# Last batch of a decoder block: expert picks moved among the cross scores, the cross query sent in parts, the last expert unit added by a one-hot product

## The reference, cut to what matters

```python
x = _layernorm(x + attn(x, ...))                       # 16 heads, low-rank q and kv, rope
x = _layernorm(x + xattn(x, ctx, ctx, mask, ...))      # q = x @ W0.T + b0, 16 heads of 16
# ffn, per batch b and expert e:
probs = softmax(einsum('bsd,ed->bse', x, choice_w))
G, I = top_k(swapaxes(probs, -1, -2), S * 2 // E)      # 256 tokens of each expert
h = silu(einsum('bekd,edf->bekf', take(x, I), w1))
out = zeros_like(x).at[b_idx, I].add(G[..., None] * einsum('bekf,efd->bekd', h, w2))
x = _layernorm(x + out)
```

## Time and profile before

| what | us |
|---|---|
| three runs | 1750.33, 1752.80, 1753.03 (median 1752.8) |
| profiled execution, its own time | 1750.27 |
| its span, first to last instruction | 1748.5 |
| mean granted TensorE clock | 0.943 of full |
| PE busy | 1545.2 (88%) |
| DVE busy | 1232.0 (70%) |
| ACT busy | 862.5 (49%) |
| POOL busy | 405.4 (23%) |

### The profile page before, as it was taken

One profiled execution on the slowest core, in us unless ns is written; L12 is line 12 of the kernel. 1 busy time (PEld: TensorE's weight loads), 2 busy tenths in 40 slices (PEclk: granted clock), 3 DMA queues, 4 the chain that ended last, 5 costly groups with the idle time before them and its releaser, 6 DMA issues. The chain is left out here.

```text
span 1748.5 us, 25995 instructions
## 1 busy us (share of the span) xinstructions
PE 1545.2 (88%) x9190; PEld 737.6 (42%) x9198; DVE 1232.0 (70%) x2551; ACT 862.5 (49%) x1611; POOL 405.4 (23%) x529
## 2 busy tenths in 40 slices
PE   7599998897999888989998989899986778999992
PEld 2222224544232255342222554322224436888872
DVE  5588854886888857888887677888865636664442
ACT  3167784353777733537777344477762231111121
POOL 5220001600200015002000250120000303666663
PEclk9699999898999998999999989899997888999997
DMA  6400001544100016350000172300002014555595
GB/s 186 124 12 1 1 2 37 153 97 104 37 1 1 1 37 183 72 135 1 1 2 29 37 191 67 105 1 2 1 1 72 23 50 123 110 111 115 111 257 120
DMA packets 101133, 118.72 MB, mean 68 GB/s; under 512 B 20365, under 2 KB 91021, under 8 KB 99853
## 3 DMA queue, kind: packets, MB, share of 16 engines
q1 hardware_dynamic: 85804, 95.81, 19.2%
q0 software_dynamic: 14208, 19.94, 6.5%
q10 hardware_dynamic: 992, 1.32, 0.3%
HBM read 65.62 MB, written 31.35 MB: 55 GB/s over the span
## 5 line engine op out<-in xcount | busy, mean ns | idle before, releaser
L1151 ACT ACTIVATE pT<-banks 128x512 f32<-128x512 f32 x1184 | 652.3, 599 | 290.5 <-PE banks L1986 165.1
L1465 DVE TENSOR_REDUCE nmf<-banks 128x1 f32<-128x1024 f32 x512 | 601.7, 1218 | 111.0 <-PE banks L1904 110.2
L1986 PE MATMUL banks<-qst,kst 99*128 99x512 bf16 x1024 | 344.2, 386 | 6.3 <-DVE nmf L1465 6.3
L1904 PE MATMUL banks<-kst,qst 96*128 96x512 bf16 x1024 | 311.7, 386 | 31.2 <-DMA qst<-oT 20.0
L2024 PE MATMUL banks<-pT,V 128*32 128x512 f32 x2048 | 274.3, 607 | 15.5 <-ACT oT L1139 12.3
L1986 PEld LDWEIGHTS banks<-qst,kst 99*128 99x128 bf16 x1024 | 96.1, 97 | 276.3 <-ACT pT L1151 173.2
L896 POOL CAST nmp<-nmf 128x16 bf16<-128x16 f32 x64 | 12.6, 196 | 774.1 <-issue 708.7
L1904 PEld LDWEIGHTS banks<-kst,qst 96*128 96x128 bf16 x1024 | 94.6, 99 | 152.2 <-DVE nmf L1465 44.6
L1321 ACT ACTIVATE kst<-banks 128x512 f32<-128x512 f32 x64 | 38.1, 597 | 204.7 <-PE banks L2350 204.6
L948 POOL DMA_INDIRECT acc_rows<-kst,tok_s x64 | 103.4, 1615 | 45.7 <-DMA acc_rows<-kst,tok_s 17.3
L1430 DVE STREAM_TRANSPOSE head_blocks<-oT 128x512 f32<-128x512 f32 x64 | 45.1, 705 | 89.5 <-ACT oT L1139 89.5
(11 more groups left out here) (244 smaller groups left out, 2168.2 us busy)
## 6 DMA issues: line engine op xcount, KB each, us to landing
qst<-q_parts SPq DMA_DIRECT2D x36, 256.0 KB, 5.1
kst<-k_parts SPq DMA_DIRECT2D x36, 256.0 KB, 7.8
qst<-in_w SPq DMA_DIRECT2D x16, 512.0 KB, 4.7
qxs<-in_w SPq DMA_DIRECT2D x16, 512.0 KB, 4.9
qst<-oT SPq DMA_DIRECT2D x60, 128.0 KB, 2.5
qxs<-oT SPq DMA_DIRECT2D x48, 128.0 KB, 2.5
xb<-in_x SPq DMA_DIRECT2D x4, 1024.0 KB, 6.8
x_rows<-z SPq DMA_DIRECT2D x4, 1024.0 KB, 8.8
```

Of the source, the lines that this page charges most:

```text
L1151: act.activation(pT[:, n % RING_P, :], PS[:, banks[what, n], :], ACT.Exp, scale=scale).then_inc(s_ex, 1)
L1465: dve.tensor_reduce(nmf[:, m % 2, j, t:t + 1], scores.rearrange("p a n -> p (a n)"), AX.X, ALU.max, negate=True).then_inc(s_smu, 1)
L1904: ins = pe.matmul(pair[:, half, :], qst[0:KQ, h, t * P:(t + 1) * P], kst[0:KQ, h, half * N:(half + 1) * N], start=True, stop=True)
L1986: ins = pe.matmul(ps, kst[0:KM, head, kc * P:(kc + 1) * P], qst[0:KM, head, cols], start=True, stop=True)
```

## The change

In the last batch: triple 0 is no longer chosen and picked ahead of cross attention. `choose` of triple 0 comes after the last "smax", its pick after "st" 21, its transposition after "st" 24; triple 1 is chosen after "st" 21, picked after "st" 31 and transposed after "st" 35. All picks use bank 1. On POOL the three gathers go behind the last split of the cross maxima. `rank_chosen` on PE goes between the cross queries 2 and 3; the subtractions of pieces 2 and 3 go into `ORDER_LAST` behind "smax" 1 and 3 (as batches 0 to 2 had them). SP sends the cross query part by part: three DMAs of a piece once its first part is taken, two at the second, one at the third.

At the end: unit 31 is not scattered. SP loads the sum of batch 3 after seven scatters, in two halves. POOL writes the token numbers 3072 to 4095 into `tokens` after unit 25, DVE compares them with the tokens of unit 31 (`spread`, two compares of 128 x 1024 after units 29 and 30), PE multiplies the one-hot tiles with the gated rows of unit 31 into banks 0 to 3 (`add_last`, 16 matmuls of 256 columns), and DVE adds the banks to the loaded sum, half by half, with statistics, power and norm by half. `hidden` of unit 31 goes behind `expert_out` of unit 30.

```diff
-ORDER_LAST = (ORDER_CROSS[:LAST_MAX + 25] + [("pick", 1)] + ORDER_CROSS[LAST_MAX + 25:LAST_MAX + 33]
-              + [("pick turned", 1)] + ORDER_CROSS[LAST_MAX + 33:])
+AFTER_ST = {21: ("pick", 0), 24: ("pick turned", 0), 31: ("pick", 1), 35: ("pick turned", 1)}
+for step in ORDER_CROSS:
+    ORDER_LAST.append(step)
+    if step == ("smax", SM_CROSS - 1):
+        ORDER_LAST.append(("choose", 0))
+    if step[0] == "st" and step[1] in AFTER_ST:
+        ORDER_LAST.append(AFTER_ST[step[1]])
+    if step == ("st", 21):
+        ORDER_LAST.append(("choose", 1))
...
 # SP, last batch
-                    for i in range(4):
-                        load_cross(i)
+                    for pair in ((0, 1), (2, 3)):
+                        for part in range(3):
+                            for i in pair:
+                                load_cross_part(i, part)
+                def load_cross_part(i, part):
+                    if part < 2:
+                        wait_apart(sp, s_xt[i], 2 * b + part + 1)
+                    else:
+                        wait_apart(sp, s_eva, at.taken("A", at.nth("qx", i) + 1))
+                    for t, term in enumerate(TERMS):
+                        if term[0] == part:
+                            sp.dma_start(rows[t:KQ:len(TERMS), :, half * N:(half + 1) * N],
+                                         xparts_at[:, i, part, :]).then_inc(s_qx[i], 16)
 # POOL: the three gathers behind split_max(..., range(4, NG)) instead of behind split_max(..., range(1))
 # ACT: cross parts in the order pair (0, 1), parts 0 1 2, then pair (2, 3)
 # DVE: route_early ends after routing_places
-                for n in range(SLOTS):
-                    choose(n)
-                take_rows(0)
-                take_choice(0)
-                scatter_tokens(0)
 # PE
+                        if order in (ORDER_AHEAD, ORDER_LAST) and n in (1, 3):
                             for i in (2, 3):
                                 subtract(at, b, i, n // 2)
...
                     cross_query(2)
+                    rank_chosen(EARLY * E, EARLY * TURNS + 2)
+                    subtracted((0, 1), 1)
                     cross_query(3)
-                    subtracted((0, 1), 1)
-                    subtracted((2, 3), 0)
-                    subtracted((2, 3), 1)
-                    rank_chosen(EARLY * E, EARLY * TURNS + 2)
-                    pick(0)
-                    pick_turned(0)
 # the end: SP
+                sp.wait_ge(s_sc[b], (E if b < EARLY else E - 1) * 32)
+                    for half in range(2):
+                        tiles = slice(half * T // 2, (half + 1) * T // 2)
+                        sp.dma_start(fin[b][:, tiles, :], rows[:, tiles, :]).then_inc(s_ah[half], 16)
 # POOL
+                if n < LAST:
+                    scatter(n)
+                if n == SPREAD_FROM - 4:
+                    pool.iota(tokens, pattern=[[1, S]], base=EARLY * S, ...)
 # DVE
+            def spread_rows(j):
+                dve.tensor_scalar(spread[:, j, :], tokens, tokf[:, 2 * k + j:2 * k + j + 1], None, ALU.is_equal)
+            def add_last(half, meanwhile=None):
+                dve.wait_ge(s_ah[half], 16)
+                for bank in (2 * half, 2 * half + 1):
+                    dve.wait_ge(s_fa, bank + 1)
+                    link_r(dve.tensor_tensor(fin[b][:, two, :], PS[:, bank, :]..., fin[b][:, two, :], ALU.add))
+                    for t in (2 * bank, 2 * bank + 1):
+                        ins = dve.bn_stats(st6[:, t, :], fin[b][:, t, :])
+                    if meanwhile is not None and bank % 2 == 0:
+                        meanwhile()
+                ...  # bn_aggr x4, + EPS, then POOL's power of the half
 # PE
+                for bank in range(4):
+                    for i in range(2):
+                        t = 2 * bank + i
+                        for j in range(2):
+                            ins = pe.matmul(PS[:, bank, i * D:(i + 1) * D], spread[:, j, t * P:(t + 1) * P],
+                                            yg[k][:, j, :], start=(j == 0), stop=(j == 1))
+                    ins.then_inc(s_fa, 1)
```

More of the change, by code:

```diff
@@ L205 @@
 UNITS = B * E
+LAST = UNITS - 1
+SPREAD_FROM = LAST - 2
 SLOTS = 3
@@ L208 @@
 WEIGHTS = 4
+PICK_BANK = 1
 def unit(n):
@@ L487, in decoder_block @@
         s_al = [sem(f"sum_loaded{i}") for i in range(B)]
+        s_ah = [sem(f"last_sum_loaded{i}") for i in range(2)]
         s_fz = sem("final_stats")
@@ L732, in load_cross @@
                                      ).then_inc(s_qx[i], 16)
+                def load_cross_part(i, part):
+                    mc, half = divmod(i, 2)
+                    rows = qxs[:, :, :] if mc == 0 else heads_of(qst, 1)
+                    if part < 2:
[6 more added lines that the diff above has]
+                                         xparts_at[:, i, part, :]).then_inc(s_qx[i], 16)
                 if b:
@@ L822, in _ @@
                     load_sum(b)
-                for half, done in enumerate((s_fv, s_fl)):
+                for half, done in enumerate((s_fv, s_fl) if b < EARLY else (s_fl, s_fv)):
                     tiles = slice(half * T // 2, (half + 1) * T // 2)
@@ L968, in batch @@
                 split_max(b, SM_SELF, NG, cross, range(4, NG))
+                if not more:
+                    pool.wait_ge(s_x2, EARLY * 32 + START)
+                    pool.wait_ge(s_tk, 1)
+                    for n in range(SLOTS):
+                        gather(n)
                 if more:
@@ L1228, in rest_of_batch @@
                 else:
-                    for i, part in ((0, 0), (1, 0), (0, 1), (1, 1), (2, 0), (3, 0), (0, 2), (1, 2),
-                                    (2, 1), (3, 1), (2, 2), (3, 2)):
-                        cross_part(at, b, i, part)
+                    for pair in ((0, 1), (2, 3)):
+                        for part in range(3):
+                            for i in pair:
+                                cross_part(at, b, i, part)
                 attention(b, ST_SELF, NG, ST_CROSS, ORDER_AHEAD if more else ORDER_LAST,
@@ L1407, in attention @@
                             assert made[0] == b * RADIX_STEPS
-                    elif what == "pick":
+                    elif what == "choose":
                         for k in range(SLOTS):
                             choose(SLOTS * n + k)
+                    elif what == "pick":
                         take_rows(n)
+                    elif what == "pick turned" and n == 0:
+                        take_choice(0)
+                        scatter_tokens(0)
                     elif what == "st" and n in divided:
@@ L1935, in attention @@
                         maximum(b, n0, n, cross)
-                        if order is ORDER_AHEAD and n in (1, 3):
+                        if order in (ORDER_AHEAD, ORDER_LAST) and n in (1, 3):
                             for i in (2, 3):
@@ L2014, in attention @@
                             pe.wait_ge(s_ave, b * 2 * NG + (NG if cross else 0) + g)
-                        if order is ORDER_LAST and n == 0:
-                            pe.wait_ge(s_pe2, 1 + START)
-                        elif order is ORDER_NEXT and n == 0:
+                        if order is ORDER_NEXT and n == 0:
                             taken_upto(at, at.nth("lg") + 1)
@@ L2391, in _ @@
                     pick_turned(q)
+                if n + 1 == LAST:
+                    hidden(LAST)
+            add_last()
 def host_arrays(i):
```

99 lines of the change are left out of this document (68 added, 31 removed).

## The result

| | us | median | before beside it | ratio, 95% interval |
|---|---|---|---|---|
| changed kernel | 1722.10 to 1727.53 (4 runs) | 1724.85 | 1752.91 | 0.9838 [0.9820, 0.9855] |
| the same, a second time | 1723.27 to 1729.31 (5 runs) | 1727.19 | 1754.44 | 0.9843 [0.9828, 0.9858] |

The change makes the kernel faster by 1.6%, 28 us; 1723.5 was forecast. The profiled execution took 1723.61 (span 1721.8, mean clock 0.955) where the one of before took 1750.27: 26.7 less.

A forecast was written before the change was run, and what follows sets the result against it. PE was taken to bound the expert units, with stalls ahead and a serial chain behind. 8.7 + 5.9 + 7.3 + 6.4 = 28.3 gave 1722.0 from the profiled run, 1724.5 with the median's offset; forecast 1723.5, range 1716 to 1731.

The forecast's parts named there:

- Step 1: Start of cross attention: part-by-part sends and later picks let the first maximum scores start at 1340.9 instead of 1349.6, -8.7.
- picks gone alone: Bound at the start of the maximum scores: with the old sends kept, their last lands at 1348.1, -1.5.
- The last links: Ahead of the first scores: ACT has the last parts at 1337.7, two sends at 1337.7 and 1338.3, landing 2.5 later.
- Step 2: POOL's queue in cross attention: gathers behind the last split end PE's waits for split maxima, -5.9, at least 4.6.
- Turn 2: PE's turn of maxima in cross attention: 15.4 us behind the start of the scores, the bias sum being the next bound.
- They hide: The gathers' six issues on POOL, some 1.25 each, are done 40 us before POOL's next work.
- Step 3: Picks in cross attention: PE no longer waits at pick 1, and two picks and transpositions remain, -7.3, between 0 and -9.
- Step 4: The end: sum loaded after the scatter of unit 30, in halves, last store done at 1742.1, -6.4, between -4.9 and -7.5.
- A: Rival at the cross query: sends don't come earlier, start gains only 1.5, time 1730.7; chance 0.07.
- B: Rival at the picks: PE still waits at pick 1 because of DVE's order, no gain there, time 1730.8; chance 0.08.
- C: Rival on PE's clock: it stays up without long idle times, so faster than forecast, 1719.5; chance 0.10.
- D: Rival on PE's clock: it doesn't rise in cross attention, 35.6 us more, time 1759, slower than before; chance 0.02.

The follow-up runs named there:

- after_again: The changed kernel unaltered, run a second time as yardstick: 1727.19, ratio 0.9843 to the kernel before.
- sends_whole: The changed kernel with the end of the kernel before and the cross query sent in whole pieces instead of part by part: 1739.85, ratio 0.9948.
- late_again: The changed kernel with POOL's gathers held until the last cross-attention group is emptied, repeated beside the unaltered changed kernel: 1722.82, ratio 0.9816.
- gathers_late: The changed kernel with one more wait, holding POOL's gathers until the last cross-attention group is emptied, first run: 1723.37, ratio 0.9843.
- gathers_behind: The kernel before with only its three gathers moved behind the last split of the cross maxima: 1748.18, ratio 0.9972.
- before_late: The kernel before with only its three gathers held until the last cross-attention group is emptied: 1748.06, ratio 0.9963.
- sends_parts: The kernel before with the cross query sent part by part, the picks left ahead of cross attention: 1745.42, ratio 0.9963.

## Why the prediction was right, point by point

The time was right (1723.5 against 1724.85), and the profiled pair differs by 26.7 where the sum said 28.3. Part of that is luck: the middle won less than forecast (the turned rows of unit 1 come 18.3 us earlier, not 22), and smaller differences made up for about half of it. By steps, from the table:

- **Step 1, start of the maximum scores, -8.7: right.** 23.02 to 15.35 is -7.7 in the first profile, to 14.49 in after_again -8.5. The 0.8 between them is PE's first row of the cross query, 6.65 us there at a granted clock of 0.55, 5.89 here at 0.62. The share of the sends that I bounded at -1.5 (picks gone alone) was -2.2. Like for like (see sends_whole) it was -2.95. The last links were as forecast: ACT's last part (10.8 behind the cross query in late_again, 11.1 forecast), then two sends and a landing.
- **Step 2, gathers out of POOL's way, -5.9: the term right, its cover wrong.** From first scores to the maxima of group 4: 22.03 to 16.16, -5.87. Turn 2 stood behind the bias sum as written. But "their six issues ... They hide" priced POOL's queue only. Run beside exponentials and picks they cost 3.6 to 3.7 us in other engines (late_again, gathers_late), and in the kernel before 6.5 us, by one profile, of the slowest of ten executions (gathers_behind against before_late). That is the step that failed. The room behind them was 24 us too, not 40.
- **Step 3, picks, -7.3: measured -4.8** (empty 2 to 7, 33.32 to 28.53). Without the gathers it is -8.5 (24.85). So the mechanism was right, no wait at either pick, and the term even small: pick groups take 5.95 and 5.68 in late_again, 0.8 and 0.5 for a pick instead of the 1.2 put down. That is 1.1 more won; the gathers' 3.7 of step 2, less this 1.1, is the shortfall (2.5 measured).
- **Step 4, the end, -6.4: measured -7.0** (27.41 to 20.40 from scatter 30). Load at 3.70 (said 3.8), landing 3.93 (said 3.9), load to end 16.7 (said 17.2). One term was wrong by half: the one-hot product takes 7.14, not 3.5, as its 16 products stand as 32 in the trace. (The 32 of the earlier trace rows are the outputs of two units, 8 products each.) It ended at 1707.27, 1.8 us ahead of the load instead of 5. The token numbers took 1.60 (said 1.0 to 1.4) and the compares 0.75 and 0.88 (said 1.1), all hidden.
- Not in the sum: -1.0 between the maxima of group 4 and empty 2, -1.1 in the expert units (within the spread between profiles given at sends_parts), and +1.0 given back between cross attention and the expert units, where the first transposes run at a low clock (3.39 instead of 1.94). Together -1.1. The -1.0 is chance: the group between empties 1 and 2 took 8.80 before, 7.28 here and 8.86 in after_again, the same kernel. Its profile is 24.7 us shorter from the cross query on than that of before, against 26.4 here. The clock over that group, in the columns of the earlier trace rows, first here, then in after_again:

```profile
1379.84:1387.12 7.28, 5.69 (x63) 2.39 (x63) 7.21 (x39) 3.59 (x9) 1.17 (x4) 1.00 0.02 4
1381.46:1390.32 8.86, 7.27 (x63) 2.60 (x63) 7.39 (x39) 3.59 (x9) 1.17 (x4) 0.81 0.01 3
```

Terms: 7.7 + 5.9 + 4.8 + 7.0 + 1.1, and 0.3 upstream, make 26.7 (26.8 by the rounded terms).

Rivals: A (sends not earlier) and B (picks wait) did not come; C (clock stays up) came by its condition, 1.00 from 1378 to 1416 and 0.68 for 0.50 at the start, but not by its 1719.5: the group with pick 1, 14.92 us long, had run at 0.66 before, so step 3 held most of that gain already. D fell by the same 1.00.

What stays open: why other engines pause beside the gathers. The rows show the pauses at once on PE (named "issue"), on DVE ("remote") and on ACT, which waits for PE; the last stand a little behind the issue of the last gather (1405.37, 0.95 long), and late_again has none at that place. The Trainium skill, "Runtime: NRT & Kernel Launch", Instruction fetch mechanics, says that each engine's code comes through a DMA queue of its own; code held up by gather packets is one guess, and no run here shows it. In either kernel the queue of instructions (packets, MB, share of 16 engines) moved two packets there, from 1396 to 1411 in after_again and from 1398 to 1411 in late_again:

```profile
q8 instruction: 2, 0.03, 1.0%
```

```profile
q8 instruction: 2, 0.03, 0.9%
```

The count is the same in both, so it decides nothing. Other causes, such as a held memory port or semaphore traffic, are as open; none was tried by itself.

The best version of the study is late_again; over two groups its ratios are 0.9843 and 0.9816, those of the changed kernel 0.9838 and 0.9843. Its trace is 2.5 to 4.2 us shorter from the cross query on. In time that is shown only in the one group in which both ran, by intervals that just overlap ([0.9828, 0.9858] and [0.9801, 0.9831]).

## What to carry to other kernels

Moving an indirect DMA off a full queue isn't free where it lands: look for a stretch in which the other engines stand anyway (here the norm behind the attention, where they cost nothing), and read the new neighbours' rows, not only the queue's. A sum on DRAM that waits for a chain of scatters can take its last addend from a one-hot product, if that is ready before the load lands; count its products as the trace counts them. And when a gain is gone, compare the distances between repeated marks (the empties of a bank) before and after: they say in which group it went.

## What the runs showed of the hardware that wasn't expected

- Six indirect gathers on POOL over 7.4 us lengthened the work of PE, ACT and DVE beside them by 3.6 us (six profiles with them there, 14.5 to 15.7 us for the two groups; three without, 10.9). In the kernel before it was 6.5 us in the one profile taken (12.29 + 8.22 against 8.80 + 5.18), part of it at a granted clock of 0.54 behind the pause.
- The same kernel's second cross group took 7.28 or 8.86 us from profile to profile, with PE's granted clock over it 1.00 or 0.81, behind the same 1.75 us wait of PE for DVE in both.
- The start of the last batch's cross query moved by 5 us between profiles of kernels that are the same up to there, more than most single effects; only times counted from it could be compared.
